# The first expert's gathered rows in two halves of 256 rows

## The chip, the cores and the metric

One core of a Trainium2 chip runs the whole program. The metric is device time in microseconds (us); smaller is better. The engines are TensorE (PE, with its weight loads as PEld), VectorE (DVE), ScalarE (ACT), GpSimd (POOL) and SyncE (SP). They run side by side and wait for one another by semaphores.

## The reference

A transformer layer in two parts. First cross attention: `x = x + attention(layernorm(x), ctx, ctx)`. Then a mixture of experts over all 8 x 256 = 2048 rows of 256 numbers:

```python
xt = x.reshape(N, M)
logits = xt @ wg
scores = jax.nn.softmax(logits, axis=-1)
topv, topi = jax.lax.top_k(scores, K)            # K = 2 of E = 8 experts
pos = jnp.sum(locs * flat, axis=-1).reshape(K, N).T
valid = pos < capacity                           # capacity = 512 rows
disp = disp.at[topi, pos_c].add(xk)
h = jax.nn.relu(jnp.einsum('ecm,emh->ech', disp, w1) + b1[:, None, :])
y = jnp.einsum('ech,ehm->ecm', h, w2) + b2[:, None, :]
out = jnp.sum(gate[..., None] * y[topi, pos_c], axis=1)
```

Each expert takes up to 512 rows, multiplies them by a 256 x 1024 matrix, applies relu, and multiplies by a 1024 x 256 matrix. The change is in this part, for the first expert.

## The kernel before

The function `attention` runs the first part batch by batch and stores the normalised rows in device memory (`xn_rows`). The function `experts` then routes, gathers and multiplies. Each engine has its own program, written out in order; what stands behind a waiting instruction on an engine waits as well.

**Routing.** VectorE and TensorE count each row's place in its expert's list and build `from_row`, the list of source rows for all slots. Two casts (lines 1242 and 1243) write the indices of experts 0 and 1 and raise `gidx_ready`.

**GpSimd** (from line 1129 on) issues four indirect gathers of 128 rows for expert 0 and four for expert 1 (line 1133), then makes three products `in_gate` (line 1156), and then starts its loop over experts: gather for expert e+2, and four scatters (line 1146) for expert e. The gathers of experts 0 and 1 wait for the indices alone; that of expert 2 waits for `gidx_ready` 3 and `xt_done`.

**One expert, e.** The 512 gathered rows lie as 4 tiles of 128 rows x 256. `turn_rows` turns them: TensorE transposes each 128 x 128 block (line 1339, 8 of them) into two PSUM banks, one for each half k of the 256 features, and raises `xt_done`. ScalarE rounds each bank to `XT_hi` (line 1178), VectorE writes the remainder `XT_lo` (line 1266). Both values together keep the precision, so that every product is made of three matmuls: hi x hi, lo x hi and hi x lo.

The hidden layer has 1024 columns, handled as C = 8 chunks of 128. `layer1(c)` makes 6 matmuls of 512 columns (line 1356: 2 halves k x 3 products) into a bank of four and raises `h_done`. ScalarE applies bias and relu to `hr` (line 1188), VectorE casts it to `h_hi` (line 1277) and makes `h_lo` (line 1279). `layer2(c)` (line 1366) makes 12 matmuls of 256 columns into two banks that hold y. The order on TensorE for an expert is layer1(0), layer1(1), layer1(2), then layer2(c) and layer1(c + 3) for c from 0 to 7; `turn_rows` of the next expert is put in after c = 4. Experts 0 and 1 are written out, 2 to 5 are in a loop, 6 and 7 are written out again.

**VectorE's order at the start of expert 0** is: split the weights (lines 1257, 1260), a few small operations for the gates, `XT_lo` (line 1266), then the first instruction of the step: a cast of the indices of expert 2, 128 x 4 (line 1272), and then `h_hi` and `h_lo` for each chunk.

**SP** waits for `xt_done` of expert e and issues the two 1 MB weight loads of expert e + 2 (lines 1115 and 1116).

The banks: 0 and 1 hold the transposed rows, 2, 3, 4 and 7 the hidden chunks, 5 and 6 the result y.

Of the kernel before, what the change touches and what calls it, by code (L numbers as in the profile page):

```python
# [6 lines left out]
P = 128  # L7
F32 = mybir.dt.float32
# [26 lines left out]
def wait_alone(eng, started, semaphore, value):  # L35


    if not isinstance(value, int):
        value = eng.to_reg(value)
    eng.wait_ge(started, 1)  # L40
    eng.wait_ge(semaphore, value)
# [972 lines left out]
def experts(nc, sem, sb, persist, out, w1, b1, w2, b2, xn_rows):  # L1014
# [60 lines left out]
    gidx_ready, sidx_ready = sem("gidx_ready"), sem("sidx_ready")  # L1075
    gathered = [[sem(f"gathered{q}_{j}") for j in range(ST)] for q in range(2)]
    scattered = [sem(f"scattered{q}") for q in range(2)]
    xt_done, xt_hi_ready, xt_lo_ready = sem("xt_done"), sem("xt_hi_ready"), sem("xt_lo_ready")
    wh_ready, wl_ready = sem("wh_ready"), sem("wl_ready")
    h_done, hr_ready, hh_ready, hl_ready = sem("h_done"), sem("hr_ready"), sem("hh_ready"), sem("hl_ready")  # L1080
    f2_part, y_ready = sem("f2_part"), sem("y_ready")

    xt_bank = ps[:, 0:2, :]
    h_bank = [ps[:, 2, :], ps[:, 3, :], ps[:, 4, :], ps[:, 7, :]]
    y_bank = [ps[:, 5, :], ps[:, 6, :]]
    out_rows = out.rearrange("b s m -> (b s) m")
# [16 lines left out]
    with block:  # L1103

        @block.sync
        def _(sp):
            def step(e, q, it):
                if static(e, E - 2):
                    return

                sp.wait_ge(wh_ready, 4 * (e + 1))
                wait_alone(sp, started, wl_ready, 4 * (e + 1))

                wait_alone(sp, started, xt_done, e + 1)
                sp.dma_start(raw1[q][:, :, :, :], w1[e + 2].rearrange("(k p) c j -> p k c j", p=P)).then_inc(weights_loaded[q], 16)
                sp.dma_start(raw2[q][:, :, :], w2[e + 2].rearrange("(p c) m -> p c m", p=P)).then_inc(weights_loaded[q], 16)
                wait_alone(sp, started, hr_ready, C * (e + 1))
                sp.dma_start(b1_sb[q][:, :], b1[e + 2].rearrange("(p c) -> p c", p=P)).then_inc(biases_loaded[q], 16)
                wait_alone(sp, started, biased, 2 * (e + 1))
                sp.dma_start(b2_bc[q][:, :], b2[bass.ds(e + 2, 1), :].broadcast_to([P, D])).then_inc(biases_loaded[q], 16)  # L1120

            steps(step)(sp)
            for q in range(2):
                sp.wait_ge(scattered[q], 16 * ST * (E // 2))

        @block.gpsimd
        def _(pool):
            def gather(e, q):
                wait_alone(pool, started, gidx_ready, e + 1)
                if not (isinstance(e, int) and e < 2):  # L1130
                    wait_alone(pool, started, xt_done, e - 1)
                for j in range(ST):
                    pool.indirect_dma_start(Xg[q][:, j, :], None, xn_rows[:, :],  # L1133
                                            bass.IndirectOffsetOnAxis(ap=gather_idx[q][:, j:j + 1], axis=0)).then_inc(gathered[q][j], 16)

            def step(e, q, it):
                if not static(e, E - 2):
                    gather(e + 2, q)
                pool.wait_ge(sidx_ready, e + 1)
                if not (isinstance(e, int) and e < 1):  # L1140

                    wait_alone(pool, started, scattered[1 - q], 16 * ST * (it + q))
                for j in range(ST):
                    wait_alone(pool, started, y_ready, ST * e + j + 1)

                    pool.indirect_dma_start(out_rows[:, :], bass.IndirectOffsetOnAxis(ap=scatter_idx[q][:, j:j + 1], axis=0),  # L1146
                                            Y[q][:, j, :], None, bounds_check=T - 1, oob_is_err=False, compute_op=ALU.add).then_inc(scattered[q], 16)


            pool.wait_ge(placed_b, 1)  # L1150
            pool.tensor_tensor(in_tile[:, :, 1, :], eq[:, :, :], iota_k[:, :].unsqueeze(2).broadcast_to([P, KT, SLOTS]), ALU.mult).then_inc(placed_k, 1)
            gather(0, 0)
            gather(1, 1)
            pool.wait_ge(gate_parts, 5)
            for n in range(3):
                pool.tensor_tensor(in_gate[:, :, n, :], eq[:, :, :], part[:, n, :].unsqueeze(2).broadcast_to([P, KT, SLOTS]), ALU.mult).then_inc(in_gate_ready, 1)
            steps(step)(pool)

        @block.scalar
        def _(act):  # L1160
            act.activation(ratio[:, :], dl_all[:, :], ACT.Exp).then_inc(ratio_ready, 1)

            def split_weights(e, q, it):

                act.wait_ge(weights_loaded[q], 32 * (it + 1))
                if not (isinstance(e, int) and e < 2):
                    act.wait_ge(f2_part, C * (e - 1))
                for k in range(2):
                    act.activation(w1_hi[q][:, k], raw1[q][:, k], ACT.Copy).then_inc(wh_ready, 1)
                for k in range(2):  # L1170
                    act.activation(w2_hi[q][:, 4 * k:4 * k + 4], raw2[q][:, 4 * k:4 * k + 4], ACT.Copy).then_inc(wh_ready, 1)

            def turn_rows(e, q):
                act.wait_ge(xt_done, e + 1)
                if not (isinstance(e, int) and e < 2):
                    act.wait_ge(h_done, C * (e - 1))
                for k in range(2):
                    act.activation(XT_hi[q][:, k, :], xt_bank[:, k, :], ACT.Copy).then_inc(xt_hi_ready, 1)

            def step(e, q, it):  # L1180
                act.wait_ge(biases_loaded[q], 32 * (it + 1))
                for c in range(C):
                    act.wait_ge(h_done, C * e + c + 1)
                    if c >= 2:
                        act.wait_ge(hl_ready, C * e + c - 1)
                    elif not (isinstance(e, int) and e < 1):
                        act.wait_ge(hl_ready, C * e + c - 1)
                    act.activation(hr[c % 2][:, :], h_bank[c % 4], ACT.Relu, bias=b1_sb[q][:, c:c + 1]).then_inc(hr_ready, 1)  # L1188
                    if c == 1 and not static(e, E - 1):
                        split_weights(e + 1, 1 - q, it + q)  # L1190
                if not static(e, E - 1):
                    turn_rows(e + 1, 1 - q)


            act.wait_ge(placed_b, 1)
            act.activation(in_tile[:, :, 0, :], eq[:, :, :], ACT.Copy, scale=iota_p[:, 0:1]).then_inc(placed_k, 1)
            split_weights(0, 0, 0)
            turn_rows(0, 0)
            steps(step)(act)

        @block.vector
        def _(dve):
# [59 lines left out]

            def turn_rows(e, q):
                for k in range(2):
                    dve.wait_ge(xt_hi_ready, 2 * e + k + 1)
                    dve.tensor_tensor(XT_lo[q][:, k, :], xt_bank[:, k, :], XT_hi[q][:, k, :].bitcast(F32), ALU.subtract).then_inc(xt_lo_ready, 1)  # L1266

            def step(e, q, it):
                if not static(e, E - 2):

                    dve.wait_ge(xt_done, e + 1)
                    dve.tensor_copy(gather_idx[q][:, :], from_row[:, bass.ds(ST * (e + 2), ST)]).then_inc(gidx_ready, 1)  # L1272
                for c in range(C):
                    dve.wait_ge(hr_ready, C * e + c + 1)
# [32 lines left out]
            for n in range(3):  # L1307
                dve.tensor_copy(part[:, n, :], left).then_inc(gate_parts, 1)
                if n < 2:
# [1 line left out]
                    dve.tensor_tensor(rest[:, n, :], left, part[:, n, :], ALU.subtract).then_inc(gate_parts, 1)  # L1311
                    left = rest[:, n, :]
                    dve.wait_ge(gate_parts, 2 * n + 2)
            turn_rows(0, 0)
            steps(step)(dve)

        @block.tensor
        def _(pe):
# [10 lines left out]
            last.then_inc(table_done, 1)  # L1329

            def turn_rows(e, q, it):
                if isinstance(e, int) and e < 1:
                    pe.wait_ge(gidx_ready, 2)
                else:
                    pe.wait_ge(xt_lo_ready, 2 * e)
                for j in range(ST):
                    pe.wait_ge(gathered[q][j], 16 * (it + 1))
                    for k in range(2):
                        last = pe.transpose(xt_bank[:, k, j * P:(j + 1) * P], Xg[q][:, j, k * P:(k + 1) * P], ident[:, :])  # L1339
                last.then_inc(xt_done, 1)  # L1340

            def step(e, q, it):
                def layer1(c):
# [6 lines left out]
                    n = 0  # L1350
                    for k in range(2):
                        if c == 0:
                            pe.wait_ge(xt_lo_ready, 2 * e + k + 1)
                        for w, a in ((w1_hi, XT_hi), (w1_lo, XT_hi), (w1_hi, XT_lo)):
                            n += 1
                            last = pe.matmul(h_bank[c % 4], w[q][:, k, c, :], a[q][:, k, :], start=(n == 1), stop=(n == 6))  # L1356
# [10 lines left out]
                                             start=(c == 0 and n == 0 and j % 2 == 0), stop=(c == C - 1 and n == 2), skip_group_check=True)  # L1367
                    last.then_inc(f2_part, 1)

                layer1(0)  # L1370
                layer1(1)
                layer1(2)
                for c in range(C):
                    layer2(c)
                    if c + 3 < C:
# [9 lines left out]
                    if c == C - 4 and not static(e, E - 1):  # L1385
                        turn_rows(e + 1, 1 - q, it + q)

            turn_rows(0, 0, 0)
            steps(step)(pe)


# [75 lines left out]
```

## Time and profile before

| | us |
|---|---|
| median of 3 runs | 475.74 (475.26 to 476.03) |
| the profiled execution, its own time | 474.79 |
| its span, first to last instruction | 473.0 |
| TensorE busy | 378.9 (80%) |
| TensorE weight loads busy | 320.8 (68%) |
| VectorE busy | 294.4 (62%) |
| GpSimd busy | 227.1 (48%) |
| ScalarE busy | 188.2 (40%) |
| mean granted clock of TensorE | 0.908 of full speed |

The attention part ends near 240 us, the routing near 255 us; the multiplications of the experts fill the rest. The page cuts the span into 40 slices of 11.8 us and gives the busy share of each engine in tenths. "PEclk" is the clock granted to TensorE: 10 tenths is 2.4 GHz, 5 tenths is 1.2 GHz. All positions below are in us from the span's start.

### The profile page before, as it was taken

The numbers are of one execution on the slowest core, as the hardware profiler recorded it, in microseconds if no ns is written. First come the engines' busy times: TensorE is split into PE (matmuls) and PEld (weight loads), VectorE is DVE, ScalarE is ACT, GpSimd is POOL, SyncE is SP. The second block draws the span as 40 slices with busy tenths as digits, with TensorE's granted clock in tenths as the row PEclk, the third lists the DMA queues.
The fourth block names the chain that finished last, engine by engine and source line by source line (L and its number), as shares of the span: only waits on it lengthen the run. The fifth ranks groups of instructions, "written<-read, shape, count | busy, mean of one in ns | idle before, by whom it ended". The sixth has DMA issues, their size and how long they took to land. (4 is left out here: it accounts for less than half of the span.)

```text
span 473.0 us, 8086 instructions
## 1 busy us (share of the span) xinstructions
PE 378.9 (80%) x3005; PEld 320.8 (68%) x3026; DVE 294.4 (62%) x614; ACT 188.2 (40%) x255; POOL 227.1 (48%) x311
## 2 busy tenths in 40 slices
PE   0566589999989898976422689999999999999970
PEld 0545467777768686664311479898989898999960
DVE  3445366776777666742269676868676777777540
ACT  3212345655555563634112252526262626262210
POOL 5773964756666662523114840717171717150504
PEclk9858799999999999988555599999999999999995
DMA  7621463606152528122110610818181818140303
GB/s 220 202 67 36 122 178 72 178 28 177 47 158 60 145 54 228 46 92 95 57 39 11 245 56 2 230 49 232 47 239 37 242 37 246 34 52 1 45 1 44
DMA packets 35735, 49.10 MB, mean 104 GB/s; under 512 B 4734, under 2 KB 31536, under 8 KB 34672
## 3 DMA queue, kind: packets, MB, share of 16 engines
q1 hardware_dynamic: 27744, 35.42, 24.7%
q0 software_dynamic: 6272, 8.57, 9.8%
q10 hardware_dynamic: 1680, 4.60, 3.0%
q8 instruction: 24, 0.39, 0.4%
q14 instruction: 15, 0.12, 0.1%
HBM read 27.57 MB, written 8.39 MB: 76 GB/s over the span
## 5 line engine op out<-in xcount | busy, mean ns | idle before, releaser
L1146 POOL DMA_INDIRECT out_dram<-Y,scatter_idx x32 | 52.0, 1624 | 109.0 <-DVE Y L1297 101.7
L1188 ACT ACTIVATE hr<-ps,b_sb 128x512 f32<-128x512 f32 x64 | 43.4, 688 | 109.0 <-PE ps L1356 72.0
L1366 PE MATMUL ps<-w_hi,h_hi 128*128 128x256 f32 x256 | 72.9, 285 | 1.6 <-DVE h_lo L1279 1.6
L1366 PE MATMUL ps<-w_lo,h_hi 128*128 128x256 f32 x256 | 72.4, 283 | 0.0
L1366 PE MATMUL ps<-w_hi,h_lo 128*128 128x256 f32 x256 | 72.4, 283 | 0.0
L596 DVE TENSOR_REDUCE nm<-ps 128x2 f32<-128x512 f32 (+1 forms) x96 | 61.8, 683 | 15.8 <-PE ps L755 9.0
L423 ACT ACTIVATE PT<-ps 128x1536 f32<-128x1536 f32 x32 | 46.4, 1451 | 26.4 <-PE ps L769 25.5
L1277 DVE CAST h_hi<-hr 128x512 fp32r<-128x512 f32 x64 | 29.1, 455 | 43.3 <-ACT hr L1188 43.1
L1356 PE MATMUL ps<-XT_hi,w_hi 128*128 128x512 f32 x128 | 51.3, 400 | 1.5 <-DVE XT_lo L1266 1.5
L1366 PEld LDWEIGHTS ps<-w_hi,h_hi 128*128 128x128 f32 x256 | 48.9, 191 | 3.8 <-DVE h_lo L1279 2.1
L1356 PE MATMUL ps<-XT_hi,w_lo 128*128 128x512 f32 x128 | 51.1, 399 | 0.0
L1356 PE MATMUL ps<-XT_lo,w_hi 128*128 128x512 f32 x128 | 50.5, 394 | 0.0
L1366 PEld LDWEIGHTS ps<-w_hi,h_lo 128*128 128x128 f32 x256 | 49.0, 191 | 1.6
L1366 PEld LDWEIGHTS ps<-w_lo,h_hi 128*128 128x128 f32 x256 | 49.0, 191 | 0.0
L752 PE MATMUL ps<-Ks,Qs 126*128 126x256 bf16 (+1 forms) x256 | 38.7, 259 | 9.1 <-issue 4.6
L1279 DVE TENSOR_TENSOR h_lo<-hr,h_hi 128x512 fp32r<-128x512 f32 x64 | 44.6, 697 | 2.2
L1133 POOL DMA_INDIRECT Xg<-xn_rows,gather_idx x32 | 35.1, 1098 | 16.1 <-issue 9.6
L752 PEld LDWEIGHTS ps<-Ks,Qs 126*128 126x128 bf16 x256 | 19.3, 101 | 19.8 <-DVE nm L596 10.2
L1356 PEld LDWEIGHTS ps<-XT_hi,w_hi 128*128 128x128 f32 x128 | 24.8, 193 | 5.6 <-issue 1.9
L1356 PEld LDWEIGHTS ps<-XT_lo,w_hi 128*128 128x128 f32 x128 | 24.5, 191 | 5.5
L1356 PEld LDWEIGHTS ps<-XT_hi,w_lo 128*128 128x128 f32 x128 | 24.7, 193 | 3.3
L785 PE MATMUL ps<-PT,V 128*32 128x256 f32 x256 | 21.1, 391 | 4.2 <-POOL PT L325 4.2
(174 smaller groups left out, 832.4 us busy)
## 6 DMA issues: line engine op xcount, KB each, us to landing
raw<-in_L_ffn_w_dram SPq DMA_DIRECT2D x12, 1024.0 KB, 7.4
raw<-in_L_ffn_w_dram ACTq DMA_DIRECT2D x4, 1024.0 KB, 5.6
Qs<-q_h SPq DMA_DIRECT2D x24, 128.0 KB, 2.4
Ks<-k_h SPq DMA_DIRECT2D x24, 128.0 KB, 2.5
c_sb<-in_ctx_dram SPq DMA_DIRECT2D x8, 256.0 KB, 2.8
Qs<-q_m SPq DMA_DIRECT2D x16, 128.0 KB, 2.5
Ks<-k_m SPq DMA_DIRECT2D x16, 128.0 KB, 2.5
xn_rows<-x2n SPq DMA_DIRECT2D x8, 256.0 KB, 2.5
```

The lines of the kernel that those rows point to most:

```text
L423: act.activation(PT[g % 2][:, :], prob_score, ACT.Exp, scale=float(HD) ** -0.5).then_inc(exp_done, 1)
L596: dve.tensor_reduce(nm[:, tile, h:h + count], max_bank[u % 2].rearrange("p (h j) -> p h j", h=count), AX_X, ALU.max, negate=True).then_inc ...
L752: pe.matmul(max_bank[u % 2][:, h * width:(h + 1) * width], Q[0:ROWS, h0 + h, tile * P:(tile + 1) * P], K[0:ROWS, h0 + h, 0:width], start=( ...
L785: pe.matmul(out, V[s % 2][:, 0, h, :], PT[g % 2][:, hh * S:(hh + 1) * S], start=True, stop=False)
L1133: pool.indirect_dma_start(Xg[q][:, j, :], None, xn_rows[:, :], bass.IndirectOffsetOnAxis(ap=gather_idx[q][:, j:j + 1], axis=0)).then_inc(g ...
L1146: pool.indirect_dma_start(out_rows[:, :], bass.IndirectOffsetOnAxis(ap=scatter_idx[q][:, j:j + 1], axis=0), Y[q][:, j, :], None, bounds_ch ...
L1188: act.activation(hr[c % 2][:, :], h_bank[c % 4], ACT.Relu, bias=b1_sb[q][:, c:c + 1]).then_inc(hr_ready, 1)
L1277: dve.tensor_copy(h_hi[c % 4][:, :], hr[c % 2][:, :]).then_inc(hh_ready, 1)
L1279: dve.tensor_tensor(h_lo[c % 4][:, :], hr[c % 2][:, :], h_hi[c % 4][:, :].bitcast(F32), ALU.subtract).then_inc(hl_ready, 1)
L1356: last = pe.matmul(h_bank[c % 4], w[q][:, k, c, :], a[q][:, k, :], start=(n == 1), stop=(n == 6))
L1366: last = pe.matmul(y_bank[j // 2][:, (j % 2) * D:(j % 2 + 1) * D], a[c % 4][:, j * P:(j + 1) * P], w[q][:, c, :], start=(c == 0 and n == 0 ...
```

## The change

Only expert 0, and of it only the rows' turning and the first three chunks of the first layer, are done in two halves of 256 rows. A half h is turned into two half banks: banks 0 and 1 for h = 0, and banks 5 and 6 (not yet in use for y) for h = 1. A new semaphore `xt_half_done` counts the halves. ScalarE and VectorE each make four operations of 256 elements in place of two of 512. TensorE's order for expert 0 becomes: turn half 0; first half of chunks 0 and 1; turn half 1; first half of chunk 2; second half of chunks 0, 1, 2; and then as before layer2(0), layer1(3) and so on. `h_done` of a chunk is raised after its second half. Counts of `xt_done` and `xt_lo_ready` for the later experts are shifted to fit. Those who waited for `xt_done` of expert 0 (SP, the gather of expert 2, the cast of line 1272) now wait for `xt_half_done` 2.

```diff
+    half_bank = [[ps[:, 0, 0:CAP // 2], ps[:, 1, 0:CAP // 2]], [ps[:, 5, 0:CAP // 2], ps[:, 6, 0:CAP // 2]]]
+    def xt_parts(e, k):
+        return 2 * e + k + (2 if e else 0)
...
-                wait_alone(sp, started, xt_done, e + 1)
+                if e == 0:
+                    wait_alone(sp, started, xt_half_done, 2)
+                else:
+                    wait_alone(sp, started, xt_done, e)
...
-            turn_rows(0, 0)
+            for h in range(2):
+                act.wait_ge(xt_half_done, h + 1)
+                for k in range(2):
+                    act.activation(XT_hi[0][:, k, h * CAP // 2:(h + 1) * CAP // 2], half_bank[h][k], ACT.Copy).then_inc(xt_hi_ready, 1)
...
-                    dve.wait_ge(xt_done, e + 1)
+                    if e == 0:
+                        dve.wait_ge(xt_half_done, 2)
+                    else:
+                        dve.wait_ge(xt_done, e)
                     dve.tensor_copy(gather_idx[q][:, :], from_row[:, bass.ds(ST * (e + 2), ST)]).then_inc(gidx_ready, 1)
...
-            turn_rows(0, 0)
+            for h in range(2):
+                for k in range(2):
+                    cols = slice(h * CAP // 2, (h + 1) * CAP // 2)
+                    dve.wait_ge(xt_hi_ready, 2 * h + k + 1)
+                    dve.tensor_tensor(XT_lo[0][:, k, cols], half_bank[h][k], XT_hi[0][:, k, cols].bitcast(F32), ALU.subtract).then_inc(xt_lo_ready, 1)
...
-                layer1(0)
-                layer1(1)
-                layer1(2)
+                def first_half(c, h):
+                    cols = slice(h * CAP // 2, (h + 1) * CAP // 2)
+                    n = 0
+                    for k in range(2):
+                        if c == 0:
+                            pe.wait_ge(xt_lo_ready, 2 * h + k + 1)
+                        for w, a in ((w1_hi, XT_hi), (w1_lo, XT_hi), (w1_hi, XT_lo)):
+                            n += 1
+                            last = pe.matmul(h_bank[c][:, cols], w[0][:, k, c, :], a[0][:, k, cols],
+                                             start=(n == 1 and h == 0), stop=(n == 6), skip_group_check=True)
+                    if h == 1:
+                        last.then_inc(h_done, 1)
+
+                def turn_half(h):
+                    for j in (2 * h, 2 * h + 1):
+                        pe.wait_ge(gathered[0][j], 16)
+                        for k in range(2):
+                            last = pe.transpose(half_bank[h][k][:, (j % 2) * P:(j % 2 + 1) * P], Xg[0][:, j, k * P:(k + 1) * P], ident[:, :])
+                    last.then_inc(xt_half_done, 1)
+
+                if e == 0:
+                    pe.wait_ge(gidx_ready, 2)
+                    turn_half(0)
+                    pe.wait_ge(wl_ready, 4)
+                    first_half(0, 0)
+                    first_half(1, 0)
+                    turn_half(1)
+                    first_half(2, 0)
+                    for c in range(3):
+                        first_half(c, 1)
+                else:
+                    layer1(0)
+                    layer1(1)
+                    layer1(2)
...
-            turn_rows(0, 0, 0)
             steps(step)(pe)
```

## Rows read from the trace of the kernel before

**Rows 1.** The page: parts 2 (tenths in 40 slices) and 4 (the chain, by line)

```profile
PE   0566589999989898976422689999999999999970
...
PEclk9858799999999999988555599999999999999995
...
PE ps L1366 19%; PE ps L1356 18%; PE ps L1339 1%; DVE in_slot L1233 1%; DVE gather_idx L1272 1%; POOL Xg L1133 1%; POOL out_dram L1146 1%; DMA Xg<-xn_rows,gather_idx 1%; POOLq L1103 0%; PE ps L1382 0%; DVE XT_lo L1266 0%; DVE eq L1229 0%; DVE Y L1297 0%; DVE Yb L1292 0%; DVE h_lo L1279 0%
```

**Rows 2.** Windows: length; busy PE, PEld, DVE, ACT, POOL (instructions); clock, DMA share, GB/s

```profile
18.38:22.34 3.96, 0.00 (x1) 0.03 (x1) 3.04 (x6) 1.12 (x2) 3.61 (x7) 0.82 0.73 199
44.99:46.41 1.42, 0.01 (x1) 0.00 (x1) 0.69 (x1) 0.60 (x1) 1.34 (x2) 1.00 0.56 142
49.62:51.70 2.08, 0.00 (x0) 0.00 (x0) 0.69 (x1) 1.94 (x2) 2.08 (x2) 0.99 0.73 198
51.70:53.97 2.27, 0.00 (x0) 0.03 (x1) 0.00 (x0) 0.00 (x0) 2.27 (x12) 0.50 0.58 158
53.97:58.53 4.56, 4.34 (x24) 3.54 (x26) 2.28 (x4) 1.45 (x1) 3.50 (x7) 0.51 0.21 58
266.29:270.16 3.87, 3.87 (x9) 3.10 (x10) 3.87 (x2) 0.69 (x1) 3.81 (x3) 0.51 0.91 372
272.46:274.07 1.61, 0.00 (x1) 0.00 (x1) 1.58 (x4) 1.61 (x3) 0.83 (x2) 1.00 0.00 0
274.07:280.00 5.93, 5.93 (x38) 5.42 (x39) 5.25 (x8) 2.78 (x4) 4.56 (x4) 1.00 0.24 68
280.00:455.00 175.00, 175.00 (x1163) 159.63 (x1163) 122.78 (x216) 70.38 (x98) 66.68 (x48) 1.00 0.40 102
```

**Rows 3.** Timeline of the join: start, us, engine, line, work, [idle before <-releaser]

```profile
261.52 0.69 PE L1339 MATMUL ps<-ident,Xg 128*128 128x128 f32 x2 [1.31 <-DMA Xg<-xn_rows,gather_idx]
...
264.83 1.08 ACT L1178 ACTIVATE XT_hi<-ps 128x512 fp32r<-128x512 f32 x2 [13.10 <-PE ps L1339]
...
265.46 1.29 DVE L1266 TENSOR_TENSOR XT_lo<-ps,XT_hi 128x512 fp32r<-128x512 f32 x2 [3.50 <-ACT XT_hi L1178]
...
266.29 0.77 PE L1356 MATMUL ps<-XT_hi,w_hi 128*128 128x512 f32 x1 [1.50 <-DVE XT_lo L1266]
...
273.32 0.69 DVE L1279 TENSOR_TENSOR h_lo<-hr,h_hi 128x512 fp32r<-128x512 f32 x1
...
274.07 0.38 PE L1366 MATMUL ps<-w_hi,h_hi 128*128 128x256 f32 x1 [1.61 <-DVE h_lo L1279]
```

**Rows 4.** Line 1272 in all (ns min/median/max), and timeline beside it

```profile
L1272 DVE CAST gather_idx<-from_row x6: 159/162/6300, 266.7 to 390.9; 128x4 int32<-128x4 f32 x6
...
266.66 6.30 DVE L1272 CAST gather_idx<-from_row 128x4 int32<-128x4 f32 x1
...
267.29 5.63 POOL L1156 TENSOR_TENSOR in_gate<-eq,part 128x1024 bf16<-128x1024 bf16 x3
```

**Rows 5.** GpSimd and VectorE TENSOR_TENSOR side by side, and operations of 256 elements

```profile
73.51 1.27 POOL L332 TENSOR_TENSOR cT_lo<-c_sb,cT_hi 128x512 fp32r<-128x512 f32 x1 [3.44 <-ACT cT_hi L401]
...
L604 DVE TENSOR_TENSOR attn<-ps,rec x16: 424/424/425, 73.6 to 224.5; 128x256 f32<-128x256 f32 x16
...
L472 ACT ACTIVATE nmT<-ps x8: 355/357/373, 39.9 to 203.0; 32x256 bf16<-32x256 f32 x8
```

**Rows 6.** Timeline of TensorE: 256 columns at the lower and upper clock

```profile
228.54 0.41 PE L862 MATMUL ps<-w_hi,aT_lo 128*128 128x256 f32 x1
228.75 0.41 PE L862 MATMUL ps<-w_lo,aT_hi 128*128 128x256 f32 x1
...
278.07 0.28 PE L1366 MATMUL ps<-w_hi,h_hi 128*128 128x256 f32 x1
278.19 0.28 PE L1366 MATMUL ps<-w_hi,h_lo 128*128 128x256 f32 x1
```

**Rows 7.** Landing of the loads of line 1115, and the next weight rounding

```profile
DMA to landing us min/median/max: 4.9/6.4/7.1
...
298.40 1.05 ACT L1169 ACTIVATE w_hi<-raw 128x1024 fp32r<-128x1024 f32 x1
```

More of the change, by code:

```diff
@@ L1077, in experts @@
     scattered = [sem(f"scattered{q}") for q in range(2)]
+    xt_half_done = sem("xt_half_done")
     xt_done, xt_hi_ready, xt_lo_ready = sem("xt_done"), sem("xt_hi_ready"), sem("xt_lo_ready")
@@ L1130, in gather @@
                 if not (isinstance(e, int) and e < 2):
-                    wait_alone(pool, started, xt_done, e - 1)
+                    if e == 2:
+                        wait_alone(pool, started, xt_half_done, 2)
+                    else:
+                        wait_alone(pool, started, xt_done, e - 2)
                 for j in range(ST):
@@ L1173, in turn_rows @@
             def turn_rows(e, q):
-                act.wait_ge(xt_done, e + 1)
+                act.wait_ge(xt_done, e)
                 if not (isinstance(e, int) and e < 2):
@@ L1264, in turn_rows @@
                 for k in range(2):
-                    dve.wait_ge(xt_hi_ready, 2 * e + k + 1)
+                    dve.wait_ge(xt_hi_ready, xt_parts(e, k) + 1)
                     dve.tensor_tensor(XT_lo[q][:, k, :], xt_bank[:, k, :], XT_hi[q][:, k, :].bitcast(F32), ALU.subtract).then_inc(xt_lo_ready, 1)
@@ L1331, in turn_rows @@
             def turn_rows(e, q, it):
[L1332 to L1335, printed above, removed]
+                pe.wait_ge(xt_lo_ready, xt_parts(e, 0))
                 for j in range(ST):
@@ L1352, in layer1 @@
                         if c == 0:
-                            pe.wait_ge(xt_lo_ready, 2 * e + k + 1)
+                            pe.wait_ge(xt_lo_ready, xt_parts(e, k) + 1)
                         for w, a in ((w1_hi, XT_hi), (w1_lo, XT_hi), (w1_hi, XT_lo)):
@@ L1368, in layer2 @@
                     last.then_inc(f2_part, 1)
-                layer1(0)
-                layer1(1)
-                layer1(2)
+                def first_half(c, h):
[26 more added lines that the diff above has]
+                        first_half(c, 1)
+                else:
+                    layer1(0)
+                    layer1(1)
+                    layer1(2)
                 for c in range(C):
```

## Prediction

> **What bounds the kernel now.** I read the page from the outside in. In its part 2 TensorE (PE) is at nine tenths or more in nearly every slice of the second half, and its clock row stands at 5 in four slices in the middle: the join between attention and experts, where TensorE is half idle and the granted clock is at the lower of its two levels, 1.2 instead of 2.4 GHz [rows 1]. The chain of part 4 goes mostly over the two matmul lines of the experts, 1366 and 1356 [rows 1]. The busy times by stretch say it more sharply: from 274.07 us on TensorE is busy for all of 5.93 us and then for all of 175.00 us at the full clock [rows 2]. So from the first matmul of the second layer (line 1366, expert 0, chunk 0) to the tail nothing but TensorE counts, and the tail hangs on its last matmul. This change can move the end in two ways only: it moves the moment at which line 1366 starts, 274.07 us, or it changes how fast TensorE runs after it.
>
> What sets 274.07? The timeline of the join shows it step by step [rows 3]. The four gathers of expert 0 end in four pairs of transposes, the second at 261.52. ScalarE (ACT) rounds when the last pair is through, at 264.83, VectorE (DVE) makes the remainders at 265.46, and TensorE starts the first layer at 266.29, having idled 1.5 us. It does 18 matmuls and stops at 272.46, then stands still for 1.61 us [rows 2]. The reason is the next VectorE row: a CAST of four elements per partition, line 1272, starts at 266.66 and takes 6.30 us. The six casts of that line have a median of 162 ns [rows 4]. Beside it GpSimd (POOL), done with a gather issue, runs the three products of line 1156 back to back from 267.29 to 272.92 [rows 4], and the cast ends at 272.96 with them. The chain names only VectorE here, because no semaphore is in it; the engine that held the cast is found by laying the two engines' times side by side. Behind the cast in VectorE's order stand h_hi and then h_lo, 273.32 to 274.01, and that remainder starts line 1366 at 274.07 [rows 3]. The start of the second layer is thus set by the end of three GpSimd products, not by TensorE's first layer.
>
> **The first layer comes earlier.** It loses a whole-block wait and gets halves. The first four transposes end at 262.21 (261.52 + 0.69) [rows 3]. A half rounding on ScalarE is not in the trace; the nearest row with 256 elements per partition is 357 ns [rows 5], two with 512 take 1.08 [rows 3], and I take 0.38. The half remainder on VectorE has the shape of line 604, 424 ns [rows 5]. So 262.25 + 0.38 + 0.04 + 0.42, and the 0.18 us that TensorE took after the first remainder (half of 1.29 after 265.46, to 266.29, [rows 3]), give a start at 263.3, against 266.29: 3 us earlier. At 1.2 GHz a matmul of 256 columns steps by 0.21 us [rows 6], so six take 1.28, two chunks end at 265.8, the second four transposes (two span 0.69, [rows 3]; I take 1.0 for four) end near 266.8, and the third chunk's first half runs to 268.0. Meanwhile ScalarE and VectorE turn the second half: 266.9 + 0.38 + 0.42, remainders ready at 267.8 and 268.2, so TensorE hardly waits. The 18 matmuls of the second half take 3.8 us at the lower clock and 2.2 us at the upper (0.12 each, [rows 6]). The clock rose 3.87 us after the start of this stream in the kernel before [rows 2], which gives 267.1 here; the first layer then ends between 270.1 (VectorE's remainder plus 2.2) and 271 (a late rise). The doubled number of matmuls and weight loads, 36 instead of 18, costs 18 x (2 x 0.12 - 0.23) = 0.2 us at most at the full clock and lies in this stretch.
>
> **Could the new remainders be caught by GpSimd too?** They start at 267.4 beside line 1156, where the remainders of before ran at 265.46 beside gather issues only. The nearest rows are line 604, the same shape with one operand in PSUM: 16 of them take 424 to 425 ns, among them the first, at 73.6, which lies inside a GpSimd TENSOR_TENSOR from 73.51 to 74.78 [rows 5]. So they are not held; price 0. What it costs if they are is rival (D).
>
> **VectorE's order after that.** Line 1272 now waits for xt_half_done 2 (266.9) and stands behind the two second remainders, so it issues at 268.2, in the middle of the three products. GpSimd's own queue doesn't wait for anything that the change moves (the gathers of expert 1 have no xt wait, gate_parts is complete before the first remainder is even waited for), so the products still run 267.29 to 272.92. The cast is held until 272.96 [rows 4]; h_hi, h_lo follow as before; line 1366 starts at 274.07 again. Expected gain of the earlier first layer: **0**. All of it becomes idle time of TensorE, from about 270.4 to 274.07: 3.7 us (3.1 to 4.0) where there were 1.61.
>
> **The queues that move.** SP's two 1 MB loads for expert 2 (lines 1115 and 1116) go out after 266.9 instead of 264.89, 2 us later; they land 4.9 to 7.1 us after issue [rows 7] and are read by ScalarE in the step of expert 1, at 298.40 [rows 7]. Cost 0; the cover is 20 us. GpSimd's gather for expert 2 waits for gidx_ready from line 1272, whose end doesn't move: 0. ScalarE gets hr 0 and 1 earlier and so begins the weight rounding of expert 1 earlier; TensorE doesn't wait for it: 0. Later experts wait on xt_done with a count lower by one, at the same transposes: 0.
>
> **What the longer idle costs.** Here is the term that isn't zero. The windows show what the clock did about earlier idles [rows 2]. TensorE idle 1.42 us (44.99 to 46.41): the clock stayed full. Idle 1.61 us (272.46 to 274.07): stayed. Idle 3.96 us (18.38 to 22.34): it fell within, to a mean of 0.82. Idle 4.35 us (49.62 to 53.97): half at the restart, and the matmuls then ran 4.56 us at half. An idle of 3.7 is nearest to 3.96, so I expect the lower level around 274.07. After a start, work at the lower level lasted 3.87 us (266.29 to 270.16) and 4.56 us (53.97 to 58.53) before the clock was back [rows 2]. At the lower level a step costs 0.21, at the upper 0.12 [rows 6], so each us there loses 1 - 0.12 / 0.213 = 0.44: **1.69** and 1.99 us. I take the first, since its instructions are nearest to these. Bounds: 0 if the clock stays; and if the fall comes just at the restart, the lower level can last as long as in the second case in all (2.27 + 4.56 = 6.83 us, [rows 2]), a loss of 2.98.
>
> **Sum.** Against the profiled execution, 474.79 (span 473.0 and 1.79 around it): 474.79 + 0 + 1.69 = 476.5. The median of the runs shown is 475.74, 0.95 above the profiled one; carried over, 477.4. A measurement of this kernel can tell about 0.2%, 0.95 us, from no change.
>
> **The rivals.**
> (A) Forecast: start of line 1366 unmoved, clock lower for 3 to 6.8 us: 477.0 to 478.7, likeliest 477.4. For it: [rows 2, 4]. 0.66.
> (B) The clock survives the idle. If the first layer ends late (271) the idle is only 3.1 us, about midway between 1.61, which did nothing, and 3.96, which did. Or the fall comes and goes inside the idle. Then nothing is left: 475.7. 0.22.
> (C) Faster: line 1272, now issued in the middle of the products, gets in when one of them ends. It is decided at the end of the first product, 267.29 + 5.63 / 3 = 269.2: the cast runs there, h_hi is issued at 270.0 with hr 0 ready and gets in at the next end, 271.1, h_lo ends 272.2, line 1366 starts at 272.25, 1.8 us earlier, with an idle short enough to keep the clock: 473.9. Against it: the cast of before was issued 0.63 us ahead of the products, met the ends of two of them and passed at neither [rows 4]. 0.07.
> The Trainium skill (SBUF — State Buffer, Who interferes with whom) speaks for (C): of a VectorE operation in a two-port mode and a GpSimd operation, the second to issue is blocked until the first finishes, so the cast should have gone after one GpSimd instruction. By that rule the time here is that of (C). The trace differs: the wait outlasted three GpSimd instructions [rows 4], and I go by it.
> (D) The new remainders are held after all, until 272.92: the second halves start at 273.0, hr 0 is ready at 274.6 and h_lo at 275.8: 1.75 us later and, with the clock down, up to 3.4: 477.5 to 479.2. Against it: [rows 5]. 0.05.
>
> **Chances.** Faster by over 0.2%: (C) and a little scatter, 0.08. Within: (B) and the part of (A) that scatter brings under 0.95 us, 0.27. Slower: the rest of (A), and (D), 0.65. The range must hold (A) and (B): 475.3 to 478.7.
>
> **What would show it.** Line 1339's second group of transposes between two groups of first-layer matmuls, first matmul near 263.3; line 1272 still ending at 272.96, now 4.8 us long; line 1366 starting at 274.1; TensorE idle over 3 us before it; the clock row at half just after 274 with 256-column steps of 0.21 us. If line 1366 starts before 273.5, (C) or something like it holds; if it starts at 274.1 at the full clock, (B). The prediction is wrong at its root if GpSimd's three products move, since everything here hangs on their end.

## The result, and the profile after

| | before | changed |
|---|---|---|
| median, 20 runs each, us | 475.37 (473.13 to 476.29) | 476.89 (475.69 to 477.95) |
| profiled execution, us (span) | 474.79 (473.0) | 476.86 (475.1) |
| ratio of the changed kernel to the kernel before | | 1.0035 (95% interval 1.0025 to 1.0045) |

The changed kernel is slower, by 1.5 us of the medians. The forecast was 477.4, in a range of 475.3 to 478.7.

The program in front of the join doesn't take the same time in every execution: the first gather of expert 0 was issued at 255.86 us before and at 256.73 in the changed kernel, and between 254.9 and 257.7 in the experiments. The experiments change nothing in front of that issue, so this scatter isn't the change's. All profiles are therefore compared by two distances that the scatter doesn't touch: from the first gather issue to the first matmul of the second layer, and from that matmul to the end of the span. Before they are 274.07 - 255.86 = 18.21 and 473.0 - 274.07 = 198.93 us. Two rows of the kernel before that this needs and [rows 3] doesn't have, the first gather issue and the matmul that follows the first 12 of the second layer:

```profile
255.86 1.78 POOL L1133 DMA_INDIRECT Xg<-xn_rows,gather_idx  x1 [6.20 <-DVE gather_idx L1243]
...
275.61 0.40 PE L1356 MATMUL ps<-XT_hi,w_hi 128*128 128x512 f32 x1
```

The timeline of the changed kernel at the join (start, us, engine, line, work, idle before and its releaser). Its lines answer to [rows 3, 4]; 1272 (the cast of four elements) is now 1290, 1156 (the three products) is 1168, 1266 (`XT_lo`) is 1336 and 1356 (the first layer) 1397 for the halves, 1279 (`h_lo`) is 1297, 1366 (the second layer) is 1385:

```profile
256.73 1.79 POOL L1145 DMA_INDIRECT Xg<-xn_rows,gather_idx  x1 [6.19 <-DVE gather_idx L1258]
...
264.13 0.55 PE L1397 MATMUL ps<-XT_hi,w_hi 128*128 128x256 f32 x1 [1.02 <-DVE XT_lo L1336]
...
268.14 5.62 POOL L1168 TENSOR_TENSOR in_gate<-eq,part 128x1024 bf16<-128x1024 bf16 x3
...
268.22 0.76 DVE L1336 TENSOR_TENSOR XT_lo<-ps,XT_hi 128x256 fp32r<-128x256 f32 x2 [3.90 <-ACT XT_hi L1213]
...
268.89 4.91 DVE L1290 CAST gather_idx<-from_row 128x4 int32<-128x4 f32 x1
...
270.84 0.28 PE L1397 MATMUL ps<-XT_lo,w_hi 128*128 128x256 f32 x1
...
274.16 0.69 DVE L1297 TENSOR_TENSOR h_lo<-hr,h_hi 128x512 fp32r<-128x512 f32 x1
...
274.91 0.58 PE L1385 MATMUL ps<-w_hi,h_hi 128*128 128x256 f32 x1 [3.79 <-DVE h_lo L1297]
275.29 0.42 PE L1385 MATMUL ps<-w_hi,h_lo 128*128 128x256 f32 x1
```

The first layer starts 7.40 us after the first gather issue, where it took 10.43 before: the 3 us that the halves were to bring are there. The cast of four elements again ends with GpSimd's three products, at 273.80, whatever was done in front of it. The second layer starts at 274.91, 18.18 us after the gather issue, where it was 18.21. Nothing has come through. The idle before it has grown from 1.61 to 3.79 us.

The windows of the changed kernel (length; busy PE, PEld, DVE, ACT, POOL; granted clock, DMA share, GB/s), to be laid beside [rows 2]:

```profile
271.12:274.91 3.79, 0.00 (x1) 0.00 (x1) 3.76 (x4) 3.79 (x5) 3.01 (x3) 0.92 1.00 418
274.91:277.64 2.73, 2.73 (x13) 2.73 (x14) 2.66 (x5) 0.69 (x1) 2.42 (x2) 0.50 0.22 57
277.64:280.50 2.86, 2.86 (x19) 2.59 (x19) 0.97 (x2) 0.69 (x1) 2.12 (x3) 0.98 0.31 92
280.50:455.00 174.50, 174.50 (x1156) 159.07 (x1155) 123.71 (x216) 69.67 (x97) 66.71 (x48) 1.00 0.40 102
```

The clock falls towards the end of the idle (mean 0.92) and stands at 0.50 for the first 12 matmuls of the second layer, which take 2.73 us. Before, the same twelve ran from 274.07 to 275.61, 1.54 us, at the full clock [rows 2]. From the second layer to the end it is 475.1 - 274.91 = 200.19 us against 198.93. That 1.26 us, and 0.03 us the other way in front of it, is all that the change did between these two profiles; the rest of their difference is the scatter in front.

### The profile page after: what moved, and what is told of

It is laid out like the page before. It is cut to its first block and busy times, and to the rows that moved or that the text cites. A ratio compares the mean times of both kernels' runs of the same rounds, so it can differ in the third digit from the quotient of the medians.

```text
span 475.1 us, 8147 instructions
## 1 busy us (share of the span) xinstructions
PE 381.6 (80%) x3044; PEld 323.5 (68%) x3044; DVE 294.1 (62%) x616; ACT 188.5 (40%) x257; POOL 226.4 (48%) x311
## 5 line engine op out<-in xcount | busy, mean ns | idle before, releaser
L1375 PE MATMUL ps<-XT_hi,w_hi 128*128 128x512 f32 x122 | 48.2, 395 | 0.0
L1375 PE MATMUL ps<-XT_hi,w_lo 128*128 128x512 f32 x122 | 48.1, 394 | 0.0
L1375 PE MATMUL ps<-XT_lo,w_hi 128*128 128x512 f32 x122 | 47.5, 390 | 0.0
L755 PE MATMUL ps<-mask,identb 128*128 128x256 bf16 (+1 forms) x96 | 31.6, 329 | 0.0
L1375 PEld LDWEIGHTS ps<-XT_lo,w_hi 128*128 128x128 f32 x122 | 23.0, 188 | 5.2
L1375 PEld LDWEIGHTS ps<-XT_hi,w_hi 128*128 128x128 f32 x122 | 23.3, 191 | 3.3
L1375 PEld LDWEIGHTS ps<-XT_hi,w_lo 128*128 128x128 f32 x122 | 23.2, 190 | 3.0
```

What stands on the lines that cost most here:

```text
L755: pe.matmul(diag, identb[:, :], mask1[:, :, :] if tile else mask0[:, :, :], start=False, stop=True, skip_group_check=True).then_inc(a_done, 1)
```

## The experiments

All were compared with the kernel before on the same chip, which stood at 475.17 in the first four and at 475.25 in the last four.

### The idle filled

```diff
                     for c in range(3):
                         first_half(c, 1)
+                    for n in range(26):
+                        pe.matmul(h_bank[3][:, 0:CAP // 2], w1_hi[0][:, 0, 0, :], XT_hi[0][:, 0, 0:CAP // 2], start=True, stop=True)
```

> The changed kernel, with 26 matmuls of 256 columns more on TensorE behind the last of the first layer's halves (operands that are there, into the bank of chunk 3, which is started anew later; they compute nothing that is used). They take 26 x 0.12 = 3.1 us of the 3.79 us that TensorE stands idle before the second layer. Theory (lower clock after the idle): the second layer starts where it starts in the changed kernel, within 0.1 us, the granted clock stays full, the first 12 matmuls of the second layer take 1.5 instead of 2.7 us, and the time falls by 1.3 us to that of the kernel before: 475.4, within 0.1%. Rival (the split itself costs, by its doubled matmuls and weight loads or by what the queues do): the time stays 1.5 us above the kernel before, or goes higher, 476.9.

474.54 us, ratio 0.9978 (0.9955 to 1.0001). Its windows over the filling, the idle that is left, and the first 12 matmuls of the second layer:

```profile
272.25:275.35 3.10, 3.10 (x26) 2.90 (x25) 3.07 (x3) 3.10 (x4) 2.52 (x2) 1.00 1.06 443
275.35:275.92 0.57, 0.00 (x2) 0.00 (x1) 0.57 (x2) 0.57 (x1) 0.37 (x1) 1.00 0.73 288
275.92:277.46 1.54, 1.54 (x13) 1.54 (x14) 1.50 (x3) 0.73 (x2) 1.24 (x2) 1.00 0.05 11
```

Work that computes nothing takes the loss away. The clock stays at 1.00, the twelve matmuls take 1.54 us again, and from the second layer to the end it is 474.9 - 275.92 = 198.98 us. The start is where it was, 18.18 us after the gather issue. The doubled number of matmuls and weight loads is still in this kernel, so it costs nothing that can be seen; the rival that blamed the split itself falls.

### How long an idle is too long

The same with 13 and with 6 matmuls of filling.

> The changed kernel with 13 matmuls of filling instead of 26 (1.6 us), so that TensorE stands idle for some 2.2 us before the second layer. The theory has no row between 1.61 us (clock kept, kernel before) and 3.79 (clock lost, changed kernel). If 2.2 us is short enough, the first 12 matmuls of the second layer step by 0.12 us and the time is that of the kernel before; if not, they step by 0.21 and the time is 1.3 us above it. I expect the first.

476.54 us, ratio 1.0027 (1.0000 to 1.0054).

> The same with 6 matmuls of filling (0.7 us), idle some 3.1 us, which is the shortest idle that the prediction allowed for. I expect the lower clock in the second layer's first matmuls and a time about 1.3 us above the kernel before, as in the changed kernel; that the clock survives would be the prediction's rival B.

477.35 us, ratio 1.0049 (1.0024 to 1.0073). The windows of the idle and of the second layer's first matmuls, with 13:

```profile
270.99:273.08 2.09, 0.00 (x1) 0.01 (x1) 2.06 (x4) 2.09 (x3) 1.31 (x2) 1.00 0.92 388
273.08:275.81 2.73, 2.73 (x13) 2.73 (x14) 2.66 (x5) 0.72 (x2) 2.42 (x2) 0.55 0.20 54
```

and with 6:

```profile
272.04:275.03 2.99, 0.00 (x0) 0.00 (x1) 2.96 (x4) 2.99 (x4) 2.21 (x2) 1.00 0.96 404
275.03:277.90 2.87, 2.87 (x13) 2.87 (x14) 2.80 (x5) 0.73 (x2) 2.56 (x2) 0.53 0.20 51
```

With 6 the clock went as I had expected. With 13 it did not: an idle of 2.09 us lost it too, though the clock was still full when work began again and fell just behind. From the second layer to the end the two take 200.42 and 200.47 us. In these profiles the clock was kept over 1.61 us and lost after 2.09. Each length has one profile, and the fall doesn't always come at the same point (in the changed kernel within the idle, mean 0.92; with 13 and with 6 behind it, the idle at 1.00), so this isn't a limit; it says that the idle of before was nearer to the edge than I took it to be.

### GpSimd's products in front of the second expert's gathers

```diff
             gather(0, 0)
-            gather(1, 1)
             pool.wait_ge(gate_parts, 5)
             for n in range(3):
                 pool.tensor_tensor(in_gate[:, :, n, :], eq[:, :, :], part[:, n, :].unsqueeze(2).broadcast_to([P, KT, SLOTS]), ALU.mult).then_inc(in_gate_ready, 1)
+            gather(1, 1)
```

In the kernel before:

> The kernel before, with GpSimd's three products made between the gathers of expert 0 and those of expert 1, not behind both. Theory (the products hold VectorE's casts): the products run from about 262.3 to 268, the cast of the next indices ends by 268 instead of 273, the first remainder of h comes about 1.1 us after hr 0, at 271.2 or so, TensorE goes from the first into the second layer without an idle, and the second layer starts at about 272.5 instead of 274.07: 1.6 us faster, 473.8. Rival (the cast waits for something else, the weight loads or the gathers): its end doesn't move with the products, and the time stays at 475.4.

473.40 us, ratio 0.9970 (0.9952 to 0.9988). In the changed kernel:

> The changed kernel with the same move of GpSimd's products. Theory: with VectorE free from 268 on the second layer starts about 1.1 us after hr 0, at 271.7 in the timeline of before, 2.4 us earlier than there; TensorE idles under 1.5 us before it and the clock stays full: 473.0, 0.8 us below the kernel before with the same move. The split is then worth its 0.8 us, which it wasn't while VectorE was held. Rival (the split costs of itself): slower than or equal to the kernel before with the move, 473.8 or more.

470.96 us, ratio 0.9916 (0.9892 to 0.9939). Once more, beside other runs of the kernel before:

> The changed kernel with GpSimd's products made between the two gathers, as in e3_after_products_early, once more beside other runs of the kernel before. There its ratio was 0.9916, 4.0 us, while its trace shows the second layer 3.05 us nearer to the first gather issue than the kernel before has it. Theory: the gain is those 3.05 us, a ratio of 0.9936, and the rest was scatter of the part before the experts; the second layer again starts 15.2 us after the first gather issue. Rival: something more is gained in front of the join or in the tail, and the ratio stays at 0.992.

472.22 us, ratio 0.9951 (0.9928 to 0.9974). Two casts are worth watching: that of the next indices (line 1272, in the changed kernel 1290) and that of `h_hi` (1277 and 1295). The timeline of the kernel before with the move:

```profile
256.22 1.78 POOL L1133 DMA_INDIRECT Xg<-xn_rows,gather_idx  x1 [6.20 <-DVE gather_idx L1243]
...
262.62 5.62 POOL L1155 TENSOR_TENSOR in_gate<-eq,part 128x1024 bf16<-128x1024 bf16 x3
...
266.93 1.35 DVE L1272 CAST gather_idx<-from_row 128x4 int32<-128x4 f32 x1
...
270.28 0.61 DVE L1277 CAST h_hi<-hr 128x512 fp32r<-128x512 f32 x1 [2.00 <-ACT hr L1188]
270.93 0.74 DVE L1279 TENSOR_TENSOR h_lo<-hr,h_hi 128x512 fp32r<-128x512 f32 x1
...
272.50 0.28 PE L1366 MATMUL ps<-w_hi,h_hi 128*128 128x256 f32 x1
```

and of the changed kernel with it (the first of its two profiles):

```profile
255.45 1.78 POOL L1145 DMA_INDIRECT Xg<-xn_rows,gather_idx  x1 [6.20 <-DVE gather_idx L1258]
...
261.86 5.62 POOL L1167 TENSOR_TENSOR in_gate<-eq,part 128x1024 bf16<-128x1024 bf16 x3
...
267.63 0.99 POOL L1145 DMA_INDIRECT Xg<-xn_rows,gather_idx  x1 [0.16 <-issue]
...
267.80 0.16 DVE L1290 CAST gather_idx<-from_row 128x4 int32<-128x4 f32 x1
...
269.40 0.43 DVE L1295 CAST h_hi<-hr 128x512 fp32r<-128x512 f32 x1 [1.45 <-ACT hr L1200]
269.86 0.69 DVE L1297 TENSOR_TENSOR h_lo<-hr,h_hi 128x512 fp32r<-128x512 f32 x1
...
270.61 0.39 PE L1385 MATMUL ps<-w_hi,h_hi 128*128 128x256 f32 x1 [0.60 <-DVE h_lo L1297]
```

The end of the cast moves with the products: in the first they end at 268.24 and the cast at 268.28; in the second they are through at 267.48, before the cast is issued, and it takes its 0.16 us. VectorE now waits for ScalarE and not for GpSimd. In the unsplit kernel TensorE goes from layer to layer without an idle, 272.50 - 256.22 = 16.28 us after the first gather issue, 1.93 us less than before. With the split it is 15.16 us, 3.05 less than before, with 0.60 us of idle and the clock full; in the second profile 15.03. So by the traces the split is worth 1.1 to 1.25 us where VectorE is free, and nothing where it isn't. By the times alone the first comparison (0.9916 against 0.9970) shows a gain and the second (0.9951) doesn't, since its interval overlaps that of the unsplit kernel. From the second layer to the end it is 198.8, 198.99 and 199.0 us, as before.

I had expected 2.4 us for the two edits together and the traces say 3.05 to 3.18: I had taken hr 0 at the time of the unsplit kernel, and it comes earlier with the halves. The first ratio says 4.0 us and the second 2.3, each plus or minus 1.1; the 3.05 lies in both intervals. Theory's 0.9936 lies in the second interval and the rival's 0.992 doesn't. The two profiles differ by 0.13 us in the first distance and 0.01 in the second, so what the first ratio has beyond 3.05 us is in neither, and I take it for scatter. With both edits the kernel is faster than the kernel before and than the changed kernel.

One thing stays open. In the kernel before the small cast was issued at 266.66, 0.63 us ahead of the first product, beside GpSimd's last gather issue:

```profile
266.32 0.95 POOL L1133 DMA_INDIRECT Xg<-xn_rows,gather_idx  x1 [0.31 <-issue]
```

Alone it would have been through at 266.82. In the second timeline above the same cast also stands beside a gather issue, that of 267.63, and takes 0.16 us. So the products' end sets the cast's end, but what kept it in the 0.63 us before the first product no run shows.

### A gap between the products

```diff
             for n in range(3):
+                if n:
+                    wait_alone(pool, started, in_gate_ready, n)
                 pool.tensor_tensor(in_gate[:, :, n, :], eq[:, :, :], part[:, n, :].unsqueeze(2).broadcast_to([P, KT, SLOTS]), ALU.mult).then_inc(in_gate_ready, 1)
```

> The changed kernel with GpSimd waiting for its own product before it starts the next one, so that there is a gap of some 0.1 us or more between the three. Theory 1 (a product that follows without a gap keeps VectorE out, one that follows after a gap doesn't): the cast of the next indices ends with the first product, near 270.1 in the timeline of the changed kernel instead of 273.8, h_hi 0 gets in at the second gap, and the second layer starts about 1.5 us earlier, with the clock full: 474 to 475. Theory 2 (the gap is too short, or VectorE is held by something that lasts over the products): the cast still ends with the third product and the time stays at 476.9 plus at most the gaps, 0.2 us.

476.19 us, ratio 1.0033 (1.0015 to 1.0050). The time agrees with theory 2, but in the trace the cast and h_hi do what theory 1 said of them; only its gain doesn't come. The timeline, the three products (least, median and longest in ns) here and in the kernel before, and the windows of the idle and of the second layer's first matmuls:

```profile
268.22 6.01 POOL L1170 TENSOR_TENSOR in_gate<-eq,part 128x1024 bf16<-128x1024 bf16 x3
...
268.40 0.76 DVE L1338 TENSOR_TENSOR XT_lo<-ps,XT_hi 128x256 fp32r<-128x256 f32 x2 [4.02 <-ACT XT_hi L1215]
...
269.07 1.10 DVE L1292 CAST gather_idx<-from_row 128x4 int32<-128x4 f32 x1
...
270.69 1.78 DVE L1297 CAST h_hi<-hr 128x512 fp32r<-128x512 f32 x1 [0.51 <-ACT hr L1202]
...
272.50 2.28 DVE L1299 TENSOR_TENSOR h_lo<-hr,h_hi 128x512 fp32r<-128x512 f32 x1
...
274.83 0.38 PE L1387 MATMUL ps<-w_hi,h_hi 128*128 128x256 f32 x1 [3.53 <-DVE h_lo L1299]
...
L1170 POOL TENSOR_TENSOR in_gate<-eq,part x3: 1902/1902/1921, 268.2 to 272.3; 128x1024 bf16<-128x1024 bf16 x3
...
L1156 POOL TENSOR_TENSOR in_gate<-eq,part x3: 1908/1915/1917, 267.3 to 271.0; 128x1024 bf16<-128x1024 bf16 x3
...
271.30:274.83 3.53, 0.00 (x0) 0.00 (x0) 3.50 (x3) 3.53 (x5) 3.24 (x3) 1.00 1.03 429
274.83:277.50 2.67, 2.67 (x14) 2.57 (x15) 2.60 (x5) 0.83 (x2) 2.37 (x2) 0.62 0.22 58
```

The three products of 1.90 to 1.92 us add up to 5.73 and take 6.01, so each gap is 0.14 us. In the kernel before they add up to 5.74 and take 5.63: the rows overlap by 0.05 us each time, so there was no gap. The 0.14 us is enough: the small cast ends at 270.17 with the first product (270.1), and h_hi, issued beside the second (to 272.2), ends at 272.47, 0.3 us behind it. Then h_lo, a TENSOR_TENSOR with both operands in SBUF, is issued at 272.50, beside the third product, and is held: that one ends at 274.23 and h_lo at 274.78, 2.28 us in place of 0.69. Three products hold three instructions in turn, and the second layer starts 17.99 us after the gather issue, only 0.2 us earlier than in the changed kernel. The clock falls behind the idle of 3.53 us (mean 0.62 over the next 2.67). The remainders of line 1338 beside the first product, with one operand in PSUM, aren't held: two in 0.76 us.

The Trainium skill (SBUF — State Buffer, Who interferes with whom) has both kinds: a VectorE cast in a two-port mode, and a VectorE operation with two SBUF inputs beside a GpSimd operation that reads SBUF, wait if the GpSimd operation was issued first, until it is done, while an operation with at most one SBUF input and outside those modes does not. The rows agree: two casts (1.10 and 1.78 us) and h_lo (2.28) waited, the remainders with one SBUF input (two in 0.76) did not, beside products that read `eq` and `part` in SBUF. Which mode the casts ran in no row shows. That the wait ends with the first GpSimd instruction holds here, with a gap of 0.14 us between them, and did not hold where they followed one another without one (4.91 us in the changed kernel, 6.30 in [rows 4]).

### The small cast later

```diff
                     dve.tensor_tensor(h_lo[c % 4][:, :], hr[c % 2][:, :], h_hi[c % 4][:, :].bitcast(F32), ALU.subtract).then_inc(hl_ready, 1)
+                    if isinstance(e, int) and e == 0 and c == 0:
+                        next_indices()
```

`next_indices` holds the wait and the cast that stood at the head of the step; the later experts keep theirs there.

> The changed kernel with the cast of the next indices (line 1290 there) moved behind h_hi and h_lo of chunk 0. Theory: it doesn't matter which of VectorE's casts is held; h_hi 0 is issued near 270.4, is held by the same products to the same moment, and the second layer starts at most 0.1 us earlier: the time stays at that of the changed kernel, 1.5 us above the kernel before. Rival (the small cast alone is what can't pass, or its place in the order is the cause): h_lo 0 ends about 1.1 us after hr 0, near 271.6, the idle before the second layer shrinks to under 1 us and the time falls below the kernel before, to 472.5.

476.50 us, ratio 1.0028 (1.0007 to 1.0049). Timeline:

```profile
266.78 5.62 POOL L1168 TENSOR_TENSOR in_gate<-eq,part 128x1024 bf16<-128x1024 bf16 x3
...
269.29 3.41 DVE L1296 CAST h_hi<-hr 128x512 fp32r<-128x512 f32 x1 [1.52 <-ACT hr L1200]
272.73 0.69 DVE L1298 TENSOR_TENSOR h_lo<-hr,h_hi 128x512 fp32r<-128x512 f32 x1
273.34 0.16 DVE L1289 CAST gather_idx<-from_row 128x4 int32<-128x4 f32 x1
```

Now h_hi is the one that is held, to 272.70, with the products ending at 272.40, and the small cast takes 0.16 us. The second layer starts 18.12 us after the gather issue: 0.06 us won. The row on which a wait is shown is only the instruction that happened to stand first.

## Why the prediction was right

**What bounds.** That two things alone could move the end, the start of the second layer and TensorE's pace after it, held in all ten profiles: from that start to the end it is 198.8 to 199.0 us where the clock stayed full and 200.2 to 200.5 where it fell.

**The earlier first layer.** Its start was forecast at 263.3 on a gather issue at 255.86, 7.4 us after; measured 7.40. Half roundings took 380 ns (I took 0.38), half remainders 420 (0.42, by line 604). TensorE was through with the first layer at 271.12, 14.4 us after the first gather issue; the forecast was 14.2 to 15.1.

**Not held by GpSimd.** The new remainders take 414 to 425 ns, two of them beside the products. Rival (D) is out, by the row that [rows 5] pointed to.

**The start unmoved.** Gain 0, measured 0.03. The runs with the products moved show that it was they that held VectorE, in the unsplit kernel and in the changed one. The run with the small cast moved shows that the order on VectorE had nothing to do with it.

**The cost of the idle.** Forecast idle 3.7 us, measured 3.79. The lower level came. Its price was the term that was somewhat off: 1.69 forecast, 1.26 in the profile of the changed kernel, 1.49 to 1.59 in the profiles of the four experiments in which the clock fell as well, 1.5 between the medians of 20 runs. I had taken 3.87 us of work at the lower level. In the changed kernel the fall came some 0.6 us before the end of the idle (mean 0.92 over 3.79 us), where it costs nothing, and only the first 2.7 us or so of the second layer ran slowly. In the four experiments it came after work had begun; by the prediction's own factor of 0.44 their 1.49 to 1.59 us are an estimated 3.4 to 3.6 us of slow work. The other part of the difference to 477.4 is the median of before, 475.37 over 20 runs in place of 475.74 over three.

**Rival (B)**, the clock survives, gave its chance to an idle of 3.1 us. The run with 2.99 us lost the clock, and so did the one with 2.09: with what the runs showed, 0.22 was too much for it. Its other case, a fall that comes and goes inside the idle, is in none of the five profiles in which the clock fell. That the clock goes after an idle as long as this one's was right, but the prediction's rows had nothing between 1.61 and 3.96 us to go by.

**Rival (C)**, a cast that gets in between two products, was refuted for the kernel as it is. With gaps its mechanism is real and its time still wrong: I had let h_lo through at 271.5, and it is held by the third product like the others.

The view that would have misled is the chain of waits, which gives the 6.3 us to VectorE's cast. It is a true row, but of an engine that was held and did no work.

## What to carry to other kernels

Before an engine is given its data earlier, find what ends last at the next meeting point; here three GpSimd products held VectorE, and 3 us won ahead of them came back as 1.5 us lost to TensorE's clock. A row much longer than its siblings of the same line is to be read beside what GpSimd does at that time, and the remedy here was to move GpSimd's block to where VectorE has mostly operations from PSUM to do: with it the split gave its gain, and the two edits together took 2.3 to 4.0 us off the kernel before by the ratios, 3.05 to 3.18 by the traces. An idle of TensorE can have a price beyond its length, so that a shorter stretch of work in front of the same wait can be worse than a longer one.

## What the runs showed of the hardware

- GpSimd's three products, in rows that overlap by 0.05 us, kept a waiting VectorE cast out over all of them (4.9 and 6.3 us for a cast that takes 0.16). With 0.14 us between them one VectorE instruction got through at each gap. That is one profile.
- At this join TensorE idled 0.57, 0.59, 0.60 and 1.61 us without losing the clock, and lost it after 2.09, 2.99, 3.53, 3.58 and 3.79 us, in four of the five only after work had begun again. A loss cost 1.3 to 1.6 us each time.
